# Lag weights of a first stage earlier in two engines' orders, with the opening and the border re-ordered

## The reference

```python
x = x + tanh(g_xattn[0]) * autocorrelation(layernorm(x), ctx, ctx)     # 9 best lags of 128, softmax
x = x + tanh(g_ffn[0])   * routed_ffn(layernorm(x))                   # base product, top 2 of 8 experts
x = x + tanh(g_xattn[1]) * cross_attention(layernorm(x), ctx, mask)   # 32 heads, 8 groups, RMS norms
x = x + tanh(g_ffn[1])   * lora_ffn(layernorm(x))
```

## Time and profile before

| | us |
|---|---|
| median of 3 runs | 821.94 (816.72 to 822.92) |
| profiled execution | 821.45 |
| its span, first to last instruction | 819.7 |
| TensorE busy, mean granted clock | 782.6 (95%), 0.983 |
| VectorE busy | 559.7 (68%) |
| ScalarE busy | 415.0 (51%) |
| GpSimd busy | 365.5 (45%) |

### The profile page before, as it was taken

How to read it: one execution, slowest core, us unless ns; L and a number is a source line. 1 busy time by engine, 2 the same in 40 slices (tenths; PEclk the granted TensorE clock), 3 DMA queues, 4 the chain that set the end, 5 groups by cost and what they waited for, 6 DMA issues and landing times.

```text
span 819.7 us, 13174 instructions
## 1 busy us (share of the span) xinstructions
PE 782.6 (95%) x4224; PEld 634.8 (77%) x4224; DVE 559.7 (68%) x1235; ACT 415.0 (51%) x1158; POOL 365.5 (45%) x428
## 2 busy tenths in 40 slices
PE   4798889988999999999999999999999999999998
PEld 2354446567888888888888888888888888888776
DVE  4676667755777666777666777666777766777774
ACT  4355545355555644555554556544555554454421
POOL 2356665656333632453354336424632643254532
PEclk9899999998999999999999999999999999999999
DMA  8200001302100300030021002000300111000002
GB/s 302 93 27 27 26 27 34 109 1 90 28 14 1 104 26 1 1 104 27 1 61 57 14 1 91 29 12 1 103 27 1 34 46 52 2 14 1 1 27 77
DMA packets 17123, 34.61 MB, mean 42 GB/s; under 512 B 2336, under 2 KB 2592, under 8 KB 16800
## 3 DMA queue, kind: packets, MB, share of 16 engines
q1 hardware_dynamic: 17056, 33.78, 12.7%
HBM read 31.67 MB, written 2.10 MB: 41 GB/s over the span
## 4 chain that ended last, share of the span: by engine, by line
PE 74%; POOL 8%; DVE 7%; issue 6%; ACT 3%; DMA 1%; SPq 1%; POOLq 0%; ACTq 0%; DVEq 0%
PE pair L837 17%; PE pair L838 17%; PE pair L839 17%; PE pair L936 4%; PE pair L949 3%; PE pair L998 3%; PE pair L850 2%; POOL qkr L515 2%; POOL probn L507 2%; PE pair L938 1%; PE pair L874 1%; PE pair L891 1%; DMA bb<-in_bb 1%; POOL wo_lo L501 1%; PE pair L878 1%
## 5 line engine op out<-in xcount | busy, mean ns | idle before, releaser
L507 POOL TENSOR_TENSOR probn<-prob,erec 128x512 f32<-128x512 f32 x64 | 66.8, 1044 | 162.1 <-DVE erec L1315 162.1
L1320 DVE TENSOR_REDUCE qkss<-qksq 128x5 f32<-128x640 f32 x64 | 52.6, 821 | 90.3 <-ACT qksq L704 90.3
L1339 DVE TENSOR_TENSOR qkn<-pair,qkr 128x640 f32<-128x640 f32 x64 | 52.7, 824 | 89.5 <-POOL qkr L515 89.5
L697 ACT ACTIVATE prob<-score,nmax 128x128 f32<-128x128 f32 x256 | 99.6, 393 | 20.4 <-DVE nmax L1302 18.7
L837 PE MATMUL pair<-wq_hi,nT_hi 128*128 128x512 f32 x256 | 107.4, 420 | 0.0
L686 ACT ACTIVATE oT_hi<-pair 128x512 fp32r<-128x512 f32 x64 | 38.1, 595 | 136.2 <-PE pair L839 136.2
L837 PE MATMUL pair<-wo_hi,oT_hi 128*128 128x512 f32 x256 | 100.8, 394 | 2.8 <-issue 2.8
L839 PE MATMUL pair<-wq_hi,nT_lo 128*128 128x512 f32 x256 | 101.4, 396 | 0.0
L838 PE MATMUL pair<-wq_lo,nT_hi 128*128 128x512 f32 x256 | 101.4, 396 | 0.0
L838 PE MATMUL pair<-wo_lo,oT_hi 128*128 128x512 f32 x256 | 100.3, 392 | 0.0
L839 PE MATMUL pair<-wo_hi,oT_lo 128*128 128x512 f32 x256 | 99.7, 389 | 0.0
(11 more groups left out here) (173 smaller groups left out, 1990.3 us busy)
## 6 DMA issues: line engine op xcount, KB each, us to landing
wq_raw<-in_wq SPq DMA_DIRECT2D x32, 256.0 KB, 3.0
wo_raw<-in_wo SPq DMA_DIRECT2D x32, 256.0 KB, 2.9
wkv_raw<-in_wkv SPq DMA_DIRECT2D x8, 512.0 KB, 4.8
ctxn<-in_ctx_n SPq DMA_DIRECT2D x8, 256.0 KB, 3.1
ctxt<-in_ctx_t SPq DMA_DIRECT2D x8, 256.0 KB, 2.7
out<-wkv_raw SPq DMA_DIRECT2D x8, 256.0 KB, 2.0
xres<-in_x SPq DMA_DIRECT2D x1, 1280.0 KB, 11.0
wbase<-in_wbase SPq DMA_DIRECT2D x1, 1024.0 KB, 8.2
```

What stands on the lines that cost most here:

```text
L507: pool.tensor_tensor(probn[:], prob[:], erec[:].unsqueeze(2).broadcast_to([P, HG, P]), ALU.mult).then_inc(normed, 1)
L697: t = act.activation(prob[:, h, :], score[:, h, :], ACT.Exp, bias=nmax[:, h:h + 1], accum_out=esum[:, h:h + 1])
L1320: dve.tensor_reduce(qkss[:], qksq[:], AX.X, ALU.add).then_inc(qk_ss, 1)
L1339: dve.tensor_tensor(qkn[:], qk_bank, qkr[:].unsqueeze(2).broadcast_to([P, HG + 1, P]), ALU.mult).then_inc(qk_nat, 1)
```

## The change

The first stage's steps keep their work; their places in the lists change. `cT_hi` and the exponentials of batch b + 1 come at the end of slot b on ScalarE, `high_rows` at the head of the next slot. On GpSimd the remainders of weights and of the turned context stand ahead of the division, `low_rows` behind `h_scale`. In the opening batch 1's transform goes to a bank of its own, and the order of transforms, copies, statistics and loads is changed. Parts of batch 7's feed-forward move from the border into slots 1 and 2 of the second stage. The diff, cut to its core; lines that begin with @@ say in words where a part stands or what was left out:

```diff
@@ SBUF: n1T takes the place of spare (2 KB a partition), spare becomes [P, D] at the end
+        def q_spectrum(b):
+            return base_bank if b == 1 else corr_bank
@@ SyncE
+                load_ctx(2)
                 load_batches(2)
+                load_ctx(3)
                 load_turned_ctx(1)
-                load_ctx(2)
                 sp.dma_start(wkv_raw[:], wkv_d[0]).then_inc(ld_wkv, 16)
...
                 for b in range(3, B):
+                    if b > 3:
+                        load_ctx(b)
                     load_turned_ctx(b - 1)
-                    load_ctx(b)
@@ GpSimd: a wait for bias_gated moves from before the loop into add_bias(0); low_wo(0, 0) waits for h_out, B too
                 def a_slot(b):
-                    low_turned_ctx(b)
-                    if has(b - 3):
-                        low_rows(b - 3)
                     if b == 3:
                         low_wkv(0)
                     if b in (4, 5):
                         for c in (2 * b - 8, 2 * b - 7):
                             low_wq(0, c)
+                    if b > 0:
+                        low_turned_ctx(b)
                     lag_weights(b)
+                    if b == 0:
+                        f_scale(2)
+                        low_turned_ctx(0)
                     if has(b - 2):
                         add_bias(b - 2)
                     if has(b - 1):
                         h_scale(b - 1)
+                    if has(b - 3):
+                        low_rows(b - 3)
                     if has(b - 2):
                         g_scale(b - 2)
                     sums(b)
-                    if has(b + 2):
+                    if b > 0 and has(b + 2):
                         f_scale(b + 2)
@@ GpSimd: g_scale(7) from the border to slot 1, low_rows(7) to slot 2
@@ ScalarE
                 def a_slot(b):
+                    if has(b - 3):
+                        high_rows(b - 3)
                     if has(b - 2):
                         copy_hw(b - 2)
-                    if b >= 1:
+                    if b >= 2:
                         act.wait_ge(q_fwd, b + 1)
                         normalise(nx[:], b + 1, f_sc, f_root, f_norm)
-                    high_turned_ctx(b)
-                    lag_exponents(b)
                     if b == 0:
-                        copy_spectrum(1)
-                        copy_swapped(1)
                         copy_quarter(1, 0)
                         copy_quarter(1, 1)
...
                     if has(b + 2):
                         copy_swapped(b + 2)
+                    if b == 0:
+                        high_turned_ctx(0)
+                        normalise(nx[:], 2, f_sc, f_root, f_norm)
+                    if b > 0:
+                        high_turned_ctx(b + 1)
+                    lag_exponents(b + 1)
+                    if b == 0:
+                        high_turned_ctx(1)
+                    if has(b + 2):
                         copy_quarter(b + 2, 0)
                         copy_quarter(b + 2, 1)
-                    if has(b - 2):
-                        high_rows(b - 2)
@@ ScalarE, ahead of the slots; the gates' tanh goes behind normalise(nx, 1)
                 copy_swapped(0)
+                copy_quarter(0, 0)
+                copy_quarter(0, 1)
+                act.wait_ge(q_fwd, 1)
+                normalise(nx[:], 1, f_sc, f_root, f_norm)
...
+                copy_spectrum(1)
+                lag_exponents(0)
+                copy_swapped(1)
@@ ScalarE, border: high_rows(4) ahead of copy_hw(5), high_rows(6) ahead of route_exponents(7);
@@ normalise(n2, 7) from the border to slot 1, high_rows(7) to slot 2
@@ TensorE: a_slot
-                    if b == 0:
-                        ctx_transform(1, 1)
-                        ctx_transform(1, 2)
-                    q_transform(b + 1)
+                    if b > 0:
+                        q_transform(b + 1)
                     turn_lags(b)
                     if has(b - 2):
                         routed_product(b - 2)
+                    if b < 2:
+                        ctx_transform(b + 2, 0)
                     lag_transforms(b)
...
                     if has(b + 2):
                         ctx_transform(b + 2, 1)
-                        ctx_transform(b + 2, 2)
                     if b == B - 2:
                         project_q(0, (0,))
                     if has(b - 2):
                         turn_out(b - 2)
+                    if has(b + 2):
+                        ctx_transform(b + 2, 2)
@@ TensorE, ahead of the slots
+                ctx_transform(0, 2)
                 correlation(0)
-                ctx_transform(0, 2)
                 ctx_transform(1, 0)
+                ctx_transform(1, 1)
+                q_transform(1)
+                ctx_transform(1, 2)
@@ TensorE, border: base_products(6) in halves around turn_out(5), turn_hw(6) ahead of inverse(7),
@@ turn_hw(7) between project_q(2) and project_kv(2)
+                    if n == 1:
+                        base_products(B - 1, (2, 3))
+                        routed_product(B - 1)
+                    if n == 2:
+                        turn_out(B - 1)
@@ VectorE: a_slot; the bias and ident become constants(), corr_product(0) ahead of f_statistics(1)
                     pick_lags(b)
+                    if b == 0:
+                        corr_product(1, 0)
+                        corr_product(1, 1)
+                        constants()
@@ VectorE, border: route(7) in halves around scale_qk(1); add_routed(7) into slot 1 of the second stage
```

More of the change, by code:

```diff
@@ L95, in flamingo_kernel @@
             kfb = early("kfb", [P, 4, D])
-            rest8, rest9, spare, wlag = (early(n, [P, CH, P]) for n in ("rest8", "rest9", "spare", "wlag"))
+            rest8, rest9, n1T, wlag = (early(n, [P, CH, P]) for n in ("rest8", "rest9", "n1T", "wlag"))
             op = [early(f"op{i}", [P, D]) for i in range(4)]
@@ L102, in flamingo_kernel @@
             ctxn = early("ctxn", [P, 2, D])
-            n1, n1T = early("n1", [P, D]), early("n1T", [P, CH, P])
+            n1, spare = early("n1", [P, D]), early("spare", [P, D])
         wo_raw = sb("wo_raw", [P, HG, D])
@@ L500, in low_wo @@
                         pool.wait_ge(w_norm, B)
+                        pool.wait_ge(h_out, B)
                     pool.tensor_tensor(wo_lo[:, h, :], wo_raw[:, h, :], wo_hi[:, h, :].bitcast(F32),
@@ L560, in slot @@
                         norm_probs(n)
+                    if n == 1:
+                        g_scale(B - 1)
                     if on(n + 2):
                         inverse_norms(n + 2)
+                    if n == 2:
+                        low_rows(B - 1)
                     if on(n) and n % B == 1:
@@ L593, in _ @@
                 low_rows(6)
-                g_scale(7)
                 norm_probs(0)
                 inverse_norms(2)
-                low_rows(7)
                 low_wkv(1)
@@ L765, in slot @@
                         high_qk(n + 1)
+                    if n == 2:
+                        high_rows(B - 1)
                     if n == CLOSING:
@@ L781, in slot @@
                         high_v(n + 2)
+                    if n == 1:
+                        normalise(n2[:], B - 1, g_sc, g_root, g_norm)
                     if on(n) and b == 1:
@@ L790, in _ @@
                 copy_swapped(0)
+                copy_quarter(0, 0)
+                copy_quarter(0, 1)
+                act.wait_ge(q_fwd, 1)
+                normalise(nx[:], 1, f_sc, f_root, f_norm)
                 act.wait_ge(ld_g, 16)
                 act.activation(gate[:], gates_in[:], ACT.Tanh).then_inc(tanhed, 1)
-                copy_quarter(0, 0)
-                act.wait_ge(q_fwd, 1)
-                normalise(nx[:], 1, f_sc, f_root, f_norm)
-                copy_quarter(0, 1)
+                copy_spectrum(1)
+                lag_exponents(0)
+                copy_swapped(1)
                 for b in range(B - 1):
                     a_slot(b)
+                high_rows(4)
                 copy_hw(5)
-                high_turned_ctx(7)
-                lag_exponents(7)
                 copy_lags(7)
@@ L819, in _ @@
                 high_v(1)
+                high_rows(6)
                 route_exponents(7)
-                high_rows(6)
-                copy_hw(7)
                 high_qk(1)
                 exponents(0)
-                normalise(n2[:], 7, g_sc, g_root, g_norm)
+                copy_hw(7)
                 squares(2)
                 high_v(2)
-                high_rows(7)
                 high_wkv(1)
@@ L842, in q_transform @@
                     pe.wait_ge(f_norm, b + 1)
-                    need(pe, picked, PICK * b - 1)
-                    pe.matmul(corr_bank, dft[:, K_FWD, :], nx[:], start=True, stop=True).then_inc(q_fwd, 1)
+                    if b >= 2:
+                        pe.wait_ge(picked, PICK * b - 1)
```

(23 more changed lines are left out.)

29 lines of the change are left out of this document (18 added, 11 removed).

## The result

| us | before | after |
|---|---|---|
| median, first comparison (4 runs each) | 819.33 (815.46 to 822.92) | 793.17 (791.53 to 793.78) |
| median, later comparison (5 rounds) | 821.45 (816.29 to 824.0) | 791.73 (790.7 to 793.23) |
| profiled execution, span | 821.45, 819.7 | 791.53, 789.7 |
| TensorE, mean granted clock | 0.983 | 1.000 |

Three executions far off the rest (1290.8 and 2738.02 of the kernel before, 981.75 of one variant, `before_busy`) are left out of all ranges and ratios; without them no median moves by more than 0.3.

What follows compares the result with a forecast made beforehand. Stalls and low clock in slots 0 to 6 and the border were taken as the bound. Terms −13.6 −0.7 +0.3 −2.6 −4.6 −5.0 = −26.2 from 821.45 gave 795.2, stated as 795.5 us, range 789 to 806.

Steps and rivals of the forecast that it cites:

- What bounds the kernel: TensorE bounds the second stage, unchanged; savings before it reach the end; slots 3 to 5 lose 4.6 us each.
- Slots 3 to 5: First stage: stall of 2.4 us and low clock disappear, 15.6 us a slot, 46.8 instead of 60.4, −13.6.
- what is late next: Slots after the change: ScalarE's nx ready at +6.5, TensorE wants it at +6.6, hidden with nothing to spare.
- Rival A: Slots 2 to 5: ScalarE's queue brings nx too late, 17.3 us a slot, 802 us in all; chance 0.15.
- The clock: TensorE's low clock in slots 0, 1, 3 to 5 and behind the border gives away 13.1 us, 1.6% of span.
- Rival B: Opening and border give nothing, pauses and low clock move elsewhere: 808 us, or 802 with half their gain; chance 0.13.
- Slot 6 and slot 2: First stage: slot 6 takes 16.0 us for 16.72, −0.7; slot 2 takes 15.8 for 15.53, +0.3.
- Opening and slots 0 and 1: First stage's start: opening with slot 0 (12.5 us for 13.71) −2.6; slot 1 15.0 for 19.58, −4.6.
- The start's step: Opening: batch 0's lag choice starts once the correlation is done, not after the gated bias; slot 0 starts 1.4 us earlier.
- Border: Border to second stage: batch 7's moved work fills TensorE's stalls, some low clock won back; −5.0 us, bounds −1.5 and −7.
- Transfers: Opening and first slots: later loads on SP's queue are issued 7 us or more before needed, costed at nothing.
- Rivals C and D: Slots: C, TensorE itself closes them, 818 us, chance 0.04; D, ScalarE's queue blocked by exponentials, 830 us, chance 0.02.

Runs made afterwards that it cites:

- before_busy: Kernel before, with unused products added on TensorE in the pauses of slots 1 and 3 to 5: 815.29 us, ratio 0.994.
- scalar_late05: Kernel after, with one unused 128x512 copy on ScalarE ahead of nx in slots 2 to 6: 793.21 us, ratio 0.9687.
- scalar_late15: Kernel after, with three unused 128x512 copies on ScalarE ahead of nx in slots 2 to 6: 797.45 us, ratio 0.9731.
- scalar_order_only: Kernel after, with GpSimd's old order back in slots 1 to 6 and ScalarE in the new order: 803.53 us, ratio 0.9803.

## Why the prediction was right, and where its sizes were off

**What bounds the kernel.** Right. Everything won ahead of the second stage reached the end: 29.93 at one of its last slots. Between slots 3 to 5 and slot 2 the forecast saw 4.6 us of stall and low clock; the slots of the kernel after show both parts. TensorE's busy time fell from 17.5 to 15.5 at the same work, 2.0, and the idle time with it, 2.6.

**Slots 3 to 5**, −13.6 forecast, −13.94 measured. Right in mechanism, as the two runs with one queue undone show, and in size: 15.6 taken, 15.49 found. The step "what is late next" was right too: `nx`, 0.3 us of slack, and it is ScalarE that must not get more work. The sign of being wrong, `nx` as what TensorE waits for, shows in the weight loads alone (1.7 us in all, in five waits), hidden under running products. Rival A is thereby measured: at 1.5 us more in ScalarE's queue it would have cost 5.7, at none nothing.

**The clock.** Against the profiled executions this is the term that was mis-sized, each time in the same direction. The forecast left allowances for low clock in slot 1 (1.2 of its 15.0; 13.84 measured), in slot 0 ("pauses before it will bring low clock again": 12.5; 11.49 measured), and expected only 1.0 of 3.4 back behind the border. The granted clock was 1.00 in all of them. Of the 3.7 us by which the profiled gain exceeds the sum, slot 1 holds 1.1 and border and first slots 0.8; slot 6 (15.48 for 16.0) holds 0.5, slot 2 (15.52 for 15.8) 0.3 and slots 3 to 5 0.3. Opening and slot 0 together hold 0.6: the start came 0.96 earlier where 1.4 was forecast, slot 0 was 1.0 shorter than worked out.

Only for slot 1 is the allowance refuted: it takes 13.83 to 13.85 at 1.00 in every profile with the new opening. In slot 0 it was a fair mean: 11.5 without low clock in three profiles, 12.9 to 13.1 with it in four. Behind the border low clock is missing in the kernel after, but it shows behind the same pauses in `scalar_late05` and `scalar_order_only`. The profiled execution of the kernel after is one without any of it, which is luck and makes 1.6 of the 3.7. Rival B, that opening and border give nothing because low clock returns elsewhere, is still refuted: where it returns in slot 0 it costs 1.5 of some 9, and the border brings 4.1 twice.

**The page against the rows.** The Trainium skill ("TensorE: Matmul & The Clock Gate", Part 1 on the HAM clock gate) gives its figure of under 1% for the ramp of a kernel's first products. The forecast carried it over to the low clock behind pauses, 8.2 at most by its estimate, and by that slots 3 to 5 would have given some 2 us less. They gave 13.94, and TensorE's busy time in them fell by 6.1 (52.60 to 46.47) at the same work. So the rows were the better guide there, and carrying the figure over was the mistake; the runs don't test what the page says of a kernel's start.

**Slot 6 and slot 2.** Slot 6 gained 1.24 where 0.7 was forecast; slot 2 didn't lengthen, since `nx`, though later, was still in time.

**Opening and slots 0 and 1**, −7.2 forecast, −8.9 by the profile, −8.6 by the medians. The start's step was half right: the bias does come out of the way (undone, it brings back a wait of 2.68), but the lag choice then waits 2.17 for TensorE's correlation, which the forecast had put 0.4 earlier. (The start itself, 13.99 here, lies anywhere between 12.48 and 14.36 in the seven profiles named above, the forecast's 13.55 among them.) The 1 us wait of inverse(0) for the late `sums(0)` came as worked out, 1.13 ahead of 28.27:

```profile
28.27 1.13 PE L893 MATMUL pair<-op,dft 128*128 128x512 f32 x2 [1.13 <-POOL op L485]
```

**Border**, −5.0 forecast, −4.1 by the medians, twice. The profile's −5.8 has 1.5 in it that came with the slots' part. The size was right within what these measurements tell; the working was only partly right, since one of the two stalls that it fills is still there, split in two.

**Transfers**, costed at nothing: right as far as the profile shows. In the slots no wait for a context shows, VectorE's one wait for `xres` (3.5) is that for the first load, and slots 2 and 3 have no room for another. It wasn't tried by itself.

**Rivals C and D** fell at once: TensorE closes the slots now, but only at 15.5, and the exponentials at the end of ScalarE's list hold it 0.96 us, not longer.

**Spread, and what is open.** Executions of the kernel before vary between 815 and 824, those of the kernel after between 791 and 794, and in both the time goes with the mean granted clock: in the later comparison 816.29 at 0.989, 821.45 at 0.983, 824.0 at 0.979; after the change 790.7 to 791.93 at 0.999 and 1.000, 793.2 and 793.23 at 0.995 and 0.997. The new order has fewer pauses of TensorE for low clock to follow. Why the same pause brings half speed in one execution and not in the next stays open. The forecast's match with the first comparison comes from this spread: its median of before lies 2.1 below the profiled execution, that of after 1.6 above its own, together the 3.7 by which the profiled gain is larger.

## What to carry to other kernels

In an in-order queue, place each step by when its input exists, and look at both queues in a chain: here either order undone took back 5.5 or 10.0 of the 15.2 us that the slots had won. Low clock behind a stall of TensorE is a chance and not a fixed price: weigh it by how often it follows such a stall, and don't read its share from one profile, since another execution of the same steps can differ by 1.5 us in one slot. Once an engine is busy throughout, add idle work of a known size to the next queue; the step at which the slot begins to grow is its slack.

## What the runs showed of the hardware

The length of a pause doesn't decide alone whether half speed follows. Pauses of TensorE in the first 200 us of the thirteen profiles:

| pause, us | half speed behind it |
|---|---|
| 1.00 and 1.01 (`scalar_late15`, slots 3 to 6), 1.12 to 1.22 (slot 1) | never |
| 1.40 to 1.42 with 0.96 soon after (second stage, nine profiles with the new border) | in two: `scalar_late05`, `scalar_order_only` |
| 1.93 (second stage, four profiles with the old border) | in two: before and `before_busy` |
| 2.03, 2.04 (slot 0) | in four of seven |
| 2.11, 2.25, 2.53 (`scalar_order_only`, slots 5, 4, 3) | only behind 2.25 |
| 2.10 (the same four profiles, second stage), 2.38 (before, slot 5) | always |
| 2.59 to 3.90 (slots 0, 1, 3 and 4 in six kernels) | always |

Where it follows, two products that take 1.02 at full speed take up to 1.91, and the slot takes about 1.5 (slot 0) or 1.2 us (slots 3 to 5) more.
